# Attention scores kept in PSUM for a third head group, paired reciprocals, and a norm shared by two engines

## The reference

```python
def xattn(q, latent_kv, Wq, Wkv_expand, Wout):       # NH = 16 heads of HD = 32
    qp = q @ Wq.T
    k, v = jnp.split(latent_kv @ Wkv_expand.T, 2, axis=-1)
    scores = jnp.einsum('bhqd,bhkd->bhqk', qh, kh) / sqrt(HD)
    scores = jnp.where(tril(ones((sq, sk))), scores, finfo.min)
    out = jnp.einsum('bhqk,bhkd->bhqd', softmax(scores), vh)
    return out @ Wout.T
x = x + xattn(layernorm(x), ctx_512, ...)
x = x + ffn(layernorm(x), ...)     # shared SwiGLU expert + top-2 of 8 routed SwiGLU experts
```

## Time and profile before

| | us |
|---|---|
| median of 3 runs (lowest, highest) | 342.38 (340.15, 342.55) |
| the profiled execution, time | 341.11 |
| its span | 339.2 |
| TensorE busy in the span | 323.4 (95%) |
| VectorE busy | 269.3 (79%) |
| ScalarE busy | 232.3 (68%) |
| GpSimd busy | 140.7 (41%) |

### The profile page before, as it was taken

The page is one execution under the profiler, slowest core; times in us unless marked ns, Lnnn a source line. Parts: engine busy times, 40 slices in busy tenths (PEclk is TensorE's granted clock), DMA queues, the critical chain, the costliest instruction groups (busy, mean ns, idle before and its releaser), DMA issues.

```text
span 339.2 us, 7025 instructions
## 1 busy us (share of the span) xinstructions
PE 323.4 (95%) x2285; PEld 279.1 (82%) x2285; DVE 269.3 (79%) x676; ACT 232.3 (68%) x581; POOL 140.7 (41%) x144
## 2 busy tenths in 40 slices
PE   7999998999999999999999999999999999999981
PEld 6898886777786798989888977888889999899981
DVE  4879779999756268885667999999999999899840
ACT  3666999999844134131225788888898999889831
POOL 3335475888842000343500008767743423432421
PEclk9999999999999999999999999999999999999998
DMA  7999400000004799697599865554555465455243
GB/s 227 376 337 380 142 3 3 3 3 0 3 2 182 266 348 363 272 308 272 220 283 242 247 242 94 122 119 85 99 116 121 85 110 129 97 90 116 46 50 44
DMA packets 31794, 53.00 MB, mean 156 GB/s; under 512 B 7440, under 2 KB 14992, under 8 KB 30736
## 3 DMA queue, kind: packets, MB, share of 16 engines
q1 hardware_dynamic: 27616, 43.34, 39.1%
q0 software_dynamic: 4144, 9.23, 15.7%
HBM read 32.22 MB, written 16.92 MB: 145 GB/s over the span
## 4 chain that ended last, share of the span: by engine, by line
PE 68%; ACT 10%; DMA 8%; DVE 5%; issue 2%; SPq 2%; POOL 2%; POOLq 1%; ACTq 0%; DVEq 0%
PE bank L563 28%; PE bank L893 19%; ACT prob L1053 6%; PE bank L917 4%; DMA out<-y_sb,dest 3%; PE bank L921 3%; DMA w_dn<-dnT 2%; PE bank L624 2%; PE bank L931 2%; PE bank L927 2%; PE bank L787 2%; PE bank L555 2%; SPq L348 1%; PE bank L773 1%; DMA act_w<-act_e 1%
## 5 line engine op out<-in xcount | busy, mean ns | idle before, releaser
L542 POOL DMA_INDIRECT out<-y_sb,dest x21 | 46.5, 2215 | 101.6 <-ACT y_sb L1223 60.3
L1297 DVE TENSOR_TENSOR gu_parts<-w_gu,gu_parts 128x704 fp32r<-128x704 f32 x84 | 77.2, 953 | 0.3 <-ACT gu_parts L1008 0.3
L1008 ACT ACTIVATE gu_parts<-w_gu 128x704 fp32r x84 | 66.0, 792 | 10.9 <-PE bank L893 10.2
L893 PE MATMUL bank<-gu_parts,xsT_hi 128*128 128x352 f32 x328 | 71.0, 338 | 0.0
L893 PEld LDWEIGHTS bank<-gu_parts,xsT_hi 128*128 128x128 f32 x328 | 54.3, 188 | 5.5 <-issue 4.1
L893 PE MATMUL bank<-gu_parts,xsT_lo 128*128 128x352 f32 x164 | 39.6, 322 | 0.0
L563 PE MATMUL bank<-x2T_hi,w_sg_lo 128*128 128x512 f32 (+1 forms) x88 | 32.6, 371 | 0.1
L563 PE MATMUL bank<-x2T_hi,w_sg_hi 128*128 128x512 f32 (+1 forms) x88 | 32.0, 363 | 0.0
L563 PE MATMUL bank<-x2T_lo,w_sg_hi 128*128 128x512 f32 (+1 forms) x88 | 31.9, 363 | 0.0
L439 POOL TENSOR_TENSOR prob<-prob,rrow 112x448 f32<-112x448 f32 x30 | 27.4, 933 | 9.9 <-DVE rrow L1347 9.8
L515 POOL DMA_INDIRECT xs_dram<-x2n,slot_i x14 | 14.4, 1026 | 37.1 <-DVE eid L1595 33.2
(11 more groups left out here) (216 smaller groups left out, 818.8 us busy)
## 6 DMA issues: line engine op xcount, KB each, us to landing
w_gu<-guT SPq DMA_DIRECT2D x8, 1408.0 KB, 9.4
xs_dram<-no_row SPq DMA_DIRECT2D x1, 5460.0 KB, 19.8
xs_in<-xs_dram SPq DMA_DIRECT2D x21, 256.0 KB, 2.9
w_dn<-dnT SPq DMA_DIRECT2D x8, 512.0 KB, 6.4
act_w<-act_e SPq DMA_DIRECT2D x19, 176.0 KB, 2.2
w_sg<-sguT SPq DMA_DIRECT2D x10, 256.0 KB, 5.1
w_dn<-dnT SPq DMA_DIRECT2D x8, 192.0 KB, 7.0
w_sd<-sdnT SPq DMA_DIRECT2D x5, 256.0 KB, 4.8
```

The lines of the kernel that those rows point to most:

```text
L542: pool.indirect_dma_start(out=out[:, :], out_offset=bass.IndirectOffsetOnAxis(ap=dest[:, i, 0:1], axis=0), in_=y_sb[i % 2][:, :], in_offse ...
L893: ins = pe.matmul(dst[:, 0:F], xsT[x_][:, c, :], gu2[w_][:, c, f0:f0 + F], start=c == 0 and n == 0, stop=c == C - 1 and n == 2)
L1008: act.activation(dst, src, ACT.Copy).then_inc(s[sem], 1)
L1297: dve.tensor_tensor(lo_, src, hi_.bitcast(F32), ALU.subtract).then_inc(s[sem], 1)
```

## The change

RP goes from 2 to 3: the masked scores of group 2 stay in bank S[2], `score[2]` is no longer used, masked(b,2) waits for no exps, and scores(b+1) waits for three groups of exps of batch b instead of two. RN = 2 takes RP's place where it meant how many groups of batch 0 VectorE normalises. From batch PAIRED = 3 on the reciprocals of groups 0 and 1, and of 2 and 3, are one instruction each, at the place of the second. For tiles 0 to 4 (NHALF = 5) the second norm's last step is cut in two: GpSimd writes columns 0 to 255 and VectorE columns 256 to 511, behind masked(b+2,0). Consumers of x2n wait for both.

```diff
-    RP = 2
+    RP = 3
+    RN = 2
...
             def apply2(n):
                 pool.wait_ge(s["rs2b"], n + 1)
-                pool.tensor_scalar(x2n[:, n, 0:H], xres[:, n, :], mv2[:, n, 0:1], rstd2[:, n, :],
-                                   ALU.subtract, ALU.mult).then_inc(s["x2n"], 1)
+                pool.tensor_scalar(x2n[:, n, 0:H // 2], xres[:, n, 0:H // 2], mv2[:, n, 0:1], rstd2[:, n, :],
+                                   ALU.subtract, ALU.mult).then_inc(s["x2n_p"], 1)
...
             pool.wait_ge(s["x2n"], NX)
+            pool.wait_ge(s["x2n_p"], NHALF)
...
             def t2(n, bank_):
                 pe.wait_ge(s["x2n"], n + 1)
+                pe.wait_ge(s["x2n_p"], min(n + 1, NHALF))
...
             def transposed(b, r):
-                if b == 0 and r < RP:
+                if b == 0 and r < RN:
                     pe.wait_ge(s["prob"], r + 1)
                 else:
-                    pe.wait_ge(s["prob_p"], R * b + r + 1 - RP)
+                    pe.wait_ge(s["prob_p"], R * b + r + 1 - RN)
...
+            def apply2_half(n):
+                dve.wait_ge(s["rs2b"], n + 1)
+                dve.tensor_scalar(x2n[:, n, H // 2:H], xres[:, n, H // 2:H], mv2[:, n, 0:1], rstd2[:, n, :],
+                                  ALU.subtract, ALU.mult).then_inc(s["x2n"], 1)
...
             def inverse(b, r):
+                if b >= PAIRED:
+                    if r % 2 == 1:
+                        dve.wait_ge(s["exp"], R * b + r + 1)
+                        dve.reciprocal(rrow[:, r - 1:r + 1, :], rowsum[:, r - 1:r + 1, :]).then_inc(s["rr"], 2)
+                    return
                 dve.wait_ge(s["exp"], R * b + r + 1)
                 dve.reciprocal(rrow[:, r, :], rowsum[:, r, :]).then_inc(s["rr"], 1)
...
                 if b + 2 < NB:
                     masked(b + 2, 0)
+                if 2 <= b < NB - 1:
+                    apply2_half(b - 2)
                 if b + 1 < NB:
                     inverse(b + 1, 3)
```

More of the change, by code:

```diff
@@ L50, in build @@
     R = P // HD
+    PAIRED = 3
     E = guT.shape[0]
@@ L62, in build @@
     NX = T // P
+    NHALF = NX - 2
     XB = (BLK, NX - BLK)
@@ L248, in build @@
         "x0 xt1 xt2 xrest wq0 wq1 wq2 wq3 wkeys wvals wo wgate ctx0 ctx1 wsg0 wsg1 wsd0 wsd1 wsd2 wegu wedn wedn_late "
-        "const zt sel zero wgpad sumg idf "
+        "const zt sel zero wgpad sumg idf x2n_p "
         "ctx_hi ctx_lo wkv_hi wkv_lo wq_hi wq_lo wo_hi wo_lo wsg_hi wsg_lo wsd_hi wsd_lo "
```

## The result

| | before | after |
|---|---|---|
| median of 20 runs each, same chip | 340.35 us (339.08 to 342.55) | 342.95 us (342.1 to 345.87) |
| profiled execution | 341.11 us | 342.96 us |

The changed kernel takes 1.0087 times as long (95% interval 1.0072 to 1.0102), which is 2.96 us of 340.35; the two medians are 2.60 apart. The forecast was +2.6 us and 344.4 us. The difference was right. The absolute time came out 1.45 lower, because the forecast stood on a base of 341.75 (the middle of 341.11 and 342.38), and twenty runs of the kernel before have a median of 340.35.

The account below looks back on a forecast made before the run. The attention stage was taken as paced by a loop through ScalarE and TensorE. Start-up +2.6 us and settled and last batches 0 gave 343.7 from 341.11 or 345.0 from 342.38, middle 344.4; 8-in-10 range 341.9 to 346.9.

Parts of the forecast that it names:

- Scores(b+1) behind exps(b,2) at start-up: Batches 0 to 2: scores wait for one more exps group; scores(1) +1.3, scores(2) +2.64, scores(3) +3.75 us.
- Batch 2 gives some back: In batch 2 part of the start-up delay is recovered: scores(4) at 60.43 for 57.80, +2.6 us, bounds 2.0 and 3.2.
- (a): Mask-and-max of group 2 writes PSUM instead of SBUF, 305 against 271 ns: +.15 us a batch on VectorE.
- (b): Exps of group 2 read PSUM, 1.32 us a group against 1.48: -.16 a batch on ScalarE, worth nothing when settled.
- GpSimd's half: Second norm: GpSimd's part goes from 2.08 us to between 1.04 and 2.08, by width 1.04; path gain 0.
- VectorE's half: Second norm's other half on VectorE costs .2 to .3 us, taken .25, ahead of masks and the probT copy.
- The tie at transpose (b,3): Settled batches: TensorE reaches v_proj at about 72.15, ScalarE releases it at 72.18; 0 to .1 a batch, taken 0.
- The pace is a loop through both: Settled batches: one loop through ScalarE's exps and probT copies and TensorE's v_proj and O sets the pace, 8.02 us a turn.
- The port lock: Second norm: VectorE's half could be held until GpSimd's own half ends; here that would cost next to nothing.
- Faster: Rival, chance .08: TensorE's waits and ScalarE's saving both count, start-up wait is swallowed; 1.4 less, 340.3 us.
- absorbed: Rival, chance .10: scores(1) and scores(2) come late, batches 2 and 3 take back all but some .5; 342.2 us.
- VectorE becomes the bound: Rival, chance .10: VectorE's norm half costs .55 or is held by GpSimd, delaying transpose (b,3); +2.5 more, 346.9 us.

Follow-up runs that it names:

- part 1 alone: Kernel before with only RP from 2 to 3, group 2 staying in PSUM, reciprocals and second norm as before: 342.81 us against 340.16, ratio 1.0075.
- The single batch: Kernel before with group 2 of batch 2 alone staying in PSUM: median 340.0 us against 340.12, ratio 1.001.
- parts 2 and 3 by themselves: Changed kernel with RP = 2, leaving only paired reciprocals and the second norm in halves: 339.94 us against 340.16, ratio 1.0002.

## Why the prediction was right

**Scores(b+1) behind exps(b,2) at start-up: right, in mechanism and size.** Predicted 34.43, 43.98, 52.88 and 60.43; measured 34.43, 43.99, 52.91 and 60.32. Undoing it in batches 0 to 2 alone took the loss away, and part 1 alone brought all of it. In the changed kernel the start-up cost 2.55 us (scores(0) to scores(4), 32.84 against 30.29).

**Batch 2 gives some back: right.** 3.8 us at scores(3) became 2.5 at scores(4), and by the way predicted: masked(3,0) at 53.95 for 54.03, the transpose behind VectorE's copy at 57.51 for 57.63. The single batch shows it cleanest: 1.37 us of wait and .02 of loss. The bounds 2.0 and 3.2 held.

**(a) and (b): right.** Mask-and-max into PSUM took 308 ns for 305; a group of exps from PSUM took 1.32 us (32.78 to 34.10), as taken.

**GpSimd's half: mis-sized.** 1.23 us, not 1.04 by width (2.08 for the whole). It stayed off the path. **VectorE's half: mis-sized.** .42 us long, and .33 from its start to the next instruction (70.67 to 71.00), not the .25 of the sum. The copy of probT came at 72.90, 2.84 behind the 70.06 of before; with 2.54 of that from the start-up it is .30 later in the batch, not .22, and the half's .08 is the difference.

**The tie at transpose (b,3): it fell on VectorE's side.** The prediction had v_proj still released by ScalarE's copy. It is not: the copy of probT 2 began at 74.03, and the earlier trace rows put v_proj .6 behind such a start, at 74.63, but v_proj started at 74.80. TensorE came late through the transpose, which had waited .32 for VectorE's copy. The price is small, though: scores(4) to v_proj(7) is 30.69 against 30.50, .05 a batch and within the 0 to .1 given. Before, TensorE had stood .16 for GpSimd in front of transpose (b,2) and about .13 in front of v_proj (71.82 to 72.18, where out_proj passes follow each other at .23), and both are gone now. The prediction took 0 for it, so this term is mis-sized by .19 in all. Part 1 by itself does not cost it (30.49), nor do parts 2 and 3 by themselves (30.48). With group 2 in PSUM and pairs together it is there with the half (30.69; 30.63 with PSUM from batch 3) and without it (30.59; 30.68 twice with PSUM from batch 3). So the half is not needed for it. The pairs, which the prediction put at 0 on the path, have a part in it together with part 1; how large a part each has is not shown.

**"The pace is a loop through both": too simple.** Moving .37 us off that loop shortened no period in the kernel before. At least two loops are within about .1 us of each other, and in the changed kernel the chain runs through VectorE. The forecast survived since it took the settled batches at nothing either way.

**The port lock: not seen on VectorE's half.** In four tiles the half began .09 to .16 us before GpSimd's half ended, which tests little: GpSimd's ran from 69.61 to 70.83 and VectorE's began at 70.67. The fifth tells more, since VectorE's lay wholly inside GpSimd's (rows of the changed kernel):

```profile
94.10 0.46 DVE L1330 TENSOR_SCALAR x2n<-xres,mv,rstd 128x256 f32<-128x256 f32 x1
```

```profile
93.87 1.23 POOL L487 TENSOR_SCALAR x2n<-xres,mv,rstd 128x256 f32<-128x256 f32 x1
```

Held until 95.10, it would have lasted a microsecond or more; it took .46, the others .41. The prediction's reason for no delay (GpSimd done before VectorE comes to it) was wrong by the .2 that GpSimd's half took longer, and nothing followed from it. The rule of the Trainium skill ("SBUF — State Buffer", "Who interferes with whom") has a tensor_scalar in a two-port mode held until GpSimd's instruction ends. No row here shows that, and none says whether this tensor_scalar ran in such a mode.

**The rivals.** Faster and absorbed needed scores(4) at 57.8 or within about .5 of it; it came at 60.32. By the absolute time alone 342.95 is nearer to the absorbed rival's 342.2 than to 344.4; it is the shifts in the trace that exclude it. VectorE becomes the bound in part: the wait is there in four batches, .32 to .38 each, but the settled batches cost .19 in all, not 2.5.

**The base.** 344.4 was built on the middle between 341.11 (one execution) and 342.38 (the median of three). More runs say 340.35. Taken with that base, the same sum gives 342.95, the measured median. That it fits to the last digit is luck: the start-up came out .05 under the 2.6 and the settled batches .19 over their 0 (2.74 in the stage), and the ratio's interval allows anything from 2.5 to 3.5 us.

## What to carry to other kernels

A buffer that is kept until a later consumer is done puts one more wait in front of its next producer. Read that wait in the first iterations too, where the producer may stand waiting for the consumer, and not only in the settled ones, where it may be hidden: here, of the seven batches that another one follows, two paid 2.5 us and five next to nothing. And where three engines are all above 90% busy in a loop, look for a second loop of nearly the same length before you shorten one: here relief on one of them gained nothing against the kernel before.

## What the runs showed of the hardware

- Halving the width of the second norm's last step (a tensor_scalar) did not halve its time. VectorE: .55 us for 128x512, .42 for 128x256. GpSimd: 2.08, 1.23. By these pairs a fixed part of about .3 us on VectorE and .4 on GpSimd is paid again by each half.
- A reciprocal of 112x8 took 199 ns, one of 112x4 took 175: there a pair is nearly as cheap as a single one.
- An exp of 112x112 that reads PSUM is followed by the next at .33 us (32.78 to 33.11 in the changed kernel), one that reads SBUF at .37 (32.81 to 33.18 before), while mask-and-max is dearer when it writes PSUM (308 ns against 268 in the changed kernel). The place of a tile moves cost from one engine to the other.
- A VectorE multiply with both inputs in SBUF was held up beside GpSimd at start-up. The one of the earlier trace rows took 1.44 us from 32.25; the next, of the same shape and with GpSimd idle, took .62. GpSimd's split of w_o ended at 33.21. In the changed kernel the first began later, at 32.38, and took 1.30: it ended at 33.68, as before (33.69). So its end went with GpSimd's and not with its own start. Before:

```profile
33.81 0.62 DVE L1357 TENSOR_TENSOR prob<-prob,rrow 112x448 f32<-112x448 f32 x1
```

```profile
30.68 2.53 POOL L461 TENSOR_TENSOR w_o_lo<-w_o,w_o_hi 128x512 fp32r<-128x512 f32 x2
```
